# Two attention layers: new order of units and transfers, causal masks on VectorE, running mean on GpSimd

## The reference, cut to what matters

```python
# x: (16, 256, 128): 16 batches of 256 tokens of 128 channels; 16 heads of 8 channels
xn = layernorm(x)
q, k, v = heads(xn @ w_qkv + b_qkv)
attn = softmax(q @ k.T / sqrt(8) + rpe_bias)          # bias of (head, t - s), layer 0
s = (attn @ v) @ w_out + b_out
g = silu(mixture_of_experts(xn))                       # top 2 of 8 experts
x = x + s * g
xn = layernorm(x)
q, k = heads(xn @ qk_w + qk_b); v = heads(xn @ v_w)    # layer 1
attn = softmax(where(causal, q @ k.T / sqrt(8), -big))
new_attn = resid[h] * attn + skip[h] * eye - centre[h] * tril(1 / (t + 1))
s = (new_attn @ v) @ cproj_w
g = silu(xn @ W.T + b + (xn @ V_r) @ C.T)
x = x + s * g
```

## Time and profile before

| what | value |
|---|---|
| median of 3 runs | 1000.07 us (997.71 to 1005.07) |
| the profiled execution | 1001.72 us, span 999.9 us |
| TensorE (PE) busy | 786.2 us, 79% of the span |
| VectorE (DVE) busy | 645.5 us, 65% |
| ScalarE (ACT) busy | 509.3 us, 51% |
| GpSimd (POOL) busy | 411.4 us, 41% |
| DMA, mean | 106 GB/s, 106.13 MB |
| mean granted TensorE clock | 0.929 of full speed |

### The profile page before, as it was taken

How to read it: one execution, slowest core, us unless ns; L and a number is a source line. 1 busy time by engine, 2 the same in 40 slices (tenths; PEclk the granted TensorE clock), 3 DMA queues, 4 the chain that set the end, 5 groups by cost and what they waited for, 6 DMA issues and landing times.

```text
span 999.9 us, 19881 instructions
## 1 busy us (share of the span) xinstructions
PE 786.2 (79%) x6259; PEld 506.5 (51%) x6278; DVE 645.5 (65%) x1137; ACT 509.3 (51%) x883; POOL 411.4 (41%) x394
## 2 busy tenths in 40 slices
PE   0894787989988998854999999525598898989984
PEld 0652444555554554422555555314476666666663
DVE  6552786887788778832655655366356767676763
ACT  1243254676677766642433433258365555555542
POOL 7006776554555454421777777673210101010000
PEclk9996899999999999986999999856799999999997
DMA  5595745444544453142212222240665646464621
GB/s 141 194 192 138 174 121 123 97 94 102 123 115 92 100 122 88 31 136 59 58 53 53 58 55 54 78 122 16 142 135 124 148 117 159 115 157 117 136 58 51
DMA packets 132671, 106.13 MB, mean 106 GB/s; under 512 B 23317, under 2 KB 124633, under 8 KB 129545
## 3 DMA queue, kind: packets, MB, share of 16 engines
q1 hardware_dynamic: 122348, 91.23, 39.8%
q0 software_dynamic: 4352, 8.99, 2.9%
q10 hardware_dynamic: 5920, 5.24, 1.7%
HBM read 54.60 MB, written 50.03 MB: 105 GB/s over the span
## 4 chain that ended last, share of the span: by engine, by line
PE 27%; DMA 10%; DVE 7%; issue 4%; ACT 4%; SPq 2%; POOL 1%; DVEq 0%; ACTq 0%; POOLq 0%
PE ps L671 8%; DMA od_d<-ev 5%; PE ps L692 3%; PE ps L1567 3%; DVE mx L1272 3%; DMA rec<-od_d 2%; PE ps L683 2%; PE ps L665 2%; PE ps L1576 1%; ACT rows L893 1%; PE ps L673 1%; PE ps L1519 1%; SPq L1113 1%; PE ps L1517 1%; PE ps L1545 1%
## 5 line engine op out<-in xcount | busy, mean ns | idle before, releaser
L1272 DVE TENSOR_REDUCE mx<-ps 128x4 f32<-128x1024 f32 (+1 forms) x224 | 268.4, 1212 | 146.8 <-PE ps L1513 69.9
L1423 ACT ACTIVATE probs<-probs 128x1024 f32<-128x1024 f32 x128 | 131.8, 1051 | 64.9 <-DVE probs L1282 63.6
L1428 ACT ACTIVATE probs<-ps 128x1024 f32<-128x1024 f32 x96 | 96.8, 1024 | 82.9 <-PE ps L1545 55.8
L1202 POOL TENSOR_TENSOR qkr<-qkf,qk 128x512 f32<-128x512 f32 x27 | 31.3, 1160 | 244.0 <-ACT qk L1392 238.4
L1230 POOL TENSOR_TENSOR probs<-probs,tabB 128x1024 f32<-128x1024 f32 x42 | 99.5, 2369 | 74.6 <-ACT probs L1435 74.6
L1511 PE MATMUL ps<-tabA,eyeb 128*128 128x512 bf16 x256 | 102.3, 399 | 25.9 <-DMA ks<-parts_d 10.9
L1567 PE MATMUL ps<-probs,vpad 128*32 128x256 f32 (+1 forms) x2048 | 118.7, 362 | 4.2 <-ACT probs L1423 3.6
L1282 DVE TENSOR_TENSOR probs<-ps,tabB 128x1024 f32<-128x1024 f32 x86 | 101.5, 1210 | 4.3 <-PE ps L1539 4.3
L1513 PE MATMUL ps<-ks,qs 96*128 96x256 bf16 x512 | 102.3, 282 | 0.0
L1539 PE MATMUL ps<-qs,ks 99*128 99x256 bf16 x512 | 77.2, 280 | 6.8 <-DMA qs<-mT 2.6
L671 PE MATMUL ps<-qs,probs 128*128 x144 | 80.9, 644 | 1.4
(11 more groups left out here) (226 smaller groups left out, 1530.1 us busy)
## 6 DMA issues: line engine op xcount, KB each, us to landing
parts_d<-qk SPq DMA_DIRECT2D x64, 192.0 KB, 4.3
qs<-parts_d SPq DMA_DIRECT2D x32, 384.0 KB, 5.0
ks<-parts_d SPq DMA_DIRECT2D x32, 384.0 KB, 6.7
parts_d<-qk SPq DMA_DIRECT2D x64, 128.0 KB, 3.2
od_d<-ev SPq DMA_DIRECT2D x64, 128.0 KB
slots_in<-probs SPq DMA_DIRECT2D x1, 4680.0 KB
probs<-slots_in SPq DMA_DIRECT2D x72, 65.0 KB, 1.8
parts_d<-qk SPq DMA_DIRECT2D x64, 64.0 KB, 1.9
```

The lines of the kernel that those rows point to most:

```text
L1272: nc.vector.tensor_reduce(mx[:, s.buf(), t, heads[0]:heads[-1] + 1], ring[:, slot].rearrange("p (h n) -> p h n", n=w), AX.X, ALU.max).then ...
L1423: nc.scalar.activation(probs[:, j, :], probs[:, j, :], ACT.Exp).then_inc(exp_done, 1)
L1428: nc.scalar.activation(probs[:, j, :], ring[:, slot], ACT.Exp).then_inc(exp_done, 1)
```

## The change

Order of units: in layer 0 four A units now lead instead of three. The value products, the projections, V and the turned maxima stand at other places. The turn comes two units before the end of the period in layer 0 (`TURN` = 14). In layer 0 the units taken aside are 0, 2, 3 instead of 0, 2, 4, and unit 3's exponential comes after unit 6's. ScalarE copies the outputs later in layer 0 (place 7) and in layer 1 at place 4, behind the first B unit's exponential. SyncE's queue is reordered in both layers.

In layer 1 the mask of B units 0 to 3 is added by VectorE in PSUM (`causal`), and ScalarE waits for it. The resid gain is now in the weights of V, the skip gain is a factor in the addition, and the centre gain is multiplied once into `share`; so one product of the tokens serves both the skip term and the running mean, and it comes at place 7 of the order instead of 6, the additions on VectorE at 8. GpSimd makes the token copy, the scale, the multiplication and addition of the running mean, the parts of the maxima and the residual addition.

```diff
@@ Units
-        self.order = [("A", 0), ("A", 1), ("A", 2)]
-        for j in range(count - 3):
-            self.order += [("B", j), ("A", j + 3)]
+        self.order = [("A", j) for j in range(lead)]
+        for j in range(count - lead):
+            self.order += [("B", j), ("A", j + lead)]
@@ attention
-    U = Units(8 if layer == 0 else 6)
+    U = Units(8, 4) if layer == 0 else Units(6, 3)
...
-    LATE = 2 if layer else 4
-    SCALE = 2 if layer else 0
-    INVERT = 7 if layer else 10
-    VALUES = {9: (0, 1)} if layer else {13: (0, 1), 15: (2, 3)}
-    ASIDE = () if layer else (0, 2, 4)
-    ORDER = tuple(range(NU)) if layer else (1, 0, 3, 2, 5, 6, 4, 7)
-    PROJECT = 10 if layer else 8
+    LATE = {2: (2, 3), 4: (4, 5)} if layer else {3: (2, 3), 6: (4, 5), 8: (6, 7)}
+    VALUES = {8: (0, 1)} if layer else {12: (0, 1)}
+    SCALE, INVERT, PROJECT = (None, 11, 11) if layer else (9, 15, 11)
+    QK, V, TURN = (3, 5, NU * 2) if layer else (1, 5, 14)
+    ASIDE = () if layer else (0, 2, 3)
+    ORDER = tuple(range(NU)) if layer else (1, 0, 2, 4, 5, 6, 3, 7)
+    A_PART, A_OUT, A_TWO, A_VAL, A_MAX = (3, 4, 4, 4, 10) if layer else (4, 7, 5, 5, 12)
+    SEQ = ((("take", 0),), (("exp", 1),), (("take", 2), ("exp", 0)), (("take", 3), ("exp", 2)), (("exp", 4),),
+           (("exp", 5),), (("exp", 6), ("exp", 3)), (("exp", 7),))
@@ SyncE, body (conditions on the step left out)
-  stacks, parts 0, outputs_out, parts 1, sums_in, outputs_in, parts 2, inverses_out, inverses_in, maxima
+  layer 0: stacks, parts 0, 1, 2, outputs_out, sums_in, outputs_in, maxima, inverses_out, inverses_in
+  layer 1: stacks, parts 0, outputs_out, parts 1, 2, sums_in, outputs_in, maxima, inverses_out, inverses_in
@@ GpSimd
+            def second_body(s):
+                if s.has():
+                    tokens(s)
+                if s.has(2):
+                    rest_one(pool, nc.gpsimd, s)
+                if s.has(-3):
+                    scale(s)
+                if s.has(2):
+                    rest_two(pool, nc.gpsimd, s)
+                if s.has(-3):
+                    running_mean(s)
+                if s.has():
+                    parts_gpsimd(pool, s)
+                if s.has(-3):
+                    residual(s)
             def body(s):
+                if s.has() and s.k >= HELP:
+                    tokens(s)
...
+                    if n == 2 and s.has():
+                        parts_gpsimd(pool, s)
@@ VectorE
             def add_shape(s):
                 dve.wait_ge(e_full, s.n(-3) + 1)
+                nc.vector.tensor_tensor_scan(cum[:], v.onesT[:], misc[:, 0:T], 0.0, ALU.mult, ALU.add).then_inc(e_evac, 1)
                 dve.wait_ge(on_done, s.n(-3) + 1)
...
-                nc.vector.tensor_tensor(cum[:], cum[:], v.share, ALU.mult).then_inc(shaped, 1)
-                dve.wait_ge(shaped, n + 1)
-                nc.vector.tensor_tensor(on[:], on[:], cum[:], ALU.add).then_inc(shaped, 1)
+                nc.vector.scalar_tensor_tensor(on[:], misc[:, 0:T], cols[:, 5:6], on[:], ALU.mult, ALU.add
+                                               ).then_inc(e_evac, 1)
+            def causal(s, j, slot):
+                dve.wait_ge(full["B"], NU * s.n(-1) + j + 1)
+                diagonal = ring[:, slot].rearrange("p (h n) -> p h n", n=T)[:, :, 0:P]
+                nc.vector.tensor_tensor(diagonal, diagonal, maskB[:].unsqueeze(1).broadcast_to([P, 4, P]), ALU.add
+                                        ).then_inc(masked, 1)
@@ ScalarE, exponential of layer 1
-                    act.wait_ge(full["B"], NU * s.n(-1) + j + 1)
+                    if j < 4:
+                        act.wait_ge(masked, 4 * s.n(-1) + j + 1)
+                    else:
+                        act.wait_ge(full["B"], NU * s.n(-1) + j + 1)
@@ TensorE
-                elif w == T:
-                    if n % 2 == 0:
-                        diagonal = o[:, T * n:T * n + 2 * T].rearrange("p (h t) -> p h t", t=T)[:, :, 0:P]
-                        nc.tensor.matmul(diagonal, eyeb[:], maskB[:].unsqueeze(1).broadcast_to([P, 2, P]),
-                                         start=True, stop=False, skip_group_check=True)
...
-                        nc.tensor.matmul(misc[:, 0:T], v.wvs[:], batch_tokens(s, -3), start=True, stop=True)
-                        nc.tensor.matmul(misc[:, T:2 * T], v.wv1[:, 1, :], batch_tokens(s, -3), start=True, stop=True
-                                         ).then_inc(e_full, 1)
+                        nc.tensor.matmul(misc[:, 0:T], v.wv1[:], batch_tokens(s, -3), start=True, stop=True).then_inc(e_full, 1)
@@ middle, GpSimd
+        nc.gpsimd.tensor_scalar(v.share, v.share, v.cols[:, 6:7], None, ALU.mult).then_inc(cleared, 1)
```

More of the change, by code:

```diff
@@ L528, in _ @@
             pe.wait_ge(copied, 4 + 4 + 13)
-            for k in range(6):
+            for k in range(7):
                 nc.tensor.matmul(ps[:, 2, k:k + 1], rowsp[:, k, :], v.ones[0:1, 0:1], start=True, stop=True)
@@ L1257, in body @@
                     rest_two(pool, nc.gpsimd, s)
-                if layer == 0 and s.has() and s.k >= HELP:
-                    parts_gpsimd(pool, s)
             if layer:
                 ahead_of[1](pool)
-                pool.wait_ge(v.cleared, 4)
-                body(first)
-            emit(pool, body)
+                pool.wait_ge(v.cleared, 5)
+                second_body(first)
+            emit(pool, second_body if layer else body)
         @block.vector
@@ L1351, in body @@
                         scale(s)
+                    if layer and pos == 8 and s.has(-3):
+                        add_shape(s)
                     if U.exists(s.k, kind):
@@ L1356, in body @@
                             add_bias(s, j, U.slot(s.k, pos))
-                    if kind == "A" and j == NU - 1 and s.has() and (layer or s.k < HELP):
+                        elif layer and j < 4:
+                            causal(s, j, U.slot(s.k, pos))
+                    if kind == "A" and j == NU - 1 and s.has() and (layer == 0 and s.k < HELP):
                         maximum_parts(s)
-                    if layer and pos == 6 and s.has(-3):
-                        add_shape(s)
                     if pos == INVERT and s.has(-2):
@@ L1448, in body @@
             def body(s):
-                if s.has():
+                if layer == 0 and s.k < HELP and s.has():
                     if s.has(-1):
@@ L1453, in body @@
                 for pos, (kind, j) in enumerate(U.order):
-                    if pos == (0 if layer else 4) and s.has(-2):
+                    if pos == A_PART and s.has(2):
+                        parts_one(s)
+                    if pos == A_OUT and s.has(-2):
                         outputs(s)
                     if kind == "B" and U.exists(s.k, kind):
-                        if j in apart(s.k):
-                            take(s, j, U.slot(s.k, pos))
-                        else:
-                            exponential(s, j, U.slot(s.k, pos))
-                        if apart(s.k) and j in (2, 4, 6):
-                            exponential(s, j - 2, 0)
-                    if pos == 1 and s.has(2):
-                        parts_one(s)
-                    if pos == 4 and s.has(2):
+                        for what, i in (SEQ[j] if apart(s.k) else (("exp", j),)):
+                            if what == "take":
+                                take(s, i, U.slot(s.k, pos))
+                            else:
+                                exponential(s, i, U.slot(s.k, pos))
+                    if pos == A_TWO and s.has(2):
                         parts_two(s)
-                    if pos == 4 and s.has():
+                    if pos == A_VAL and s.has():
                         values(s)
+                    if pos == A_MAX and s.has():
+                        max_rows(s)
                 if layer and s.has(-3):
@@ L1474, in body @@
                     act.dma_start(v.wdn, v.down_w.rearrange("e (c i) h -> i e c h", c=2)).then_inc(v.w_load, 16)
-                if s.has():
+                if A_MAX >= len(U.order) and s.has():
                     max_rows(s)
@@ L1615, in body @@
                         mm.then_inc(y_full, 1)
+                    if pos == TURN and s.has():
+                        turn_maxima(s)
                     if U.exists(s.k, kind):
```

151 lines of the change are left out of this document (86 added, 65 removed).

## The result

| kernel | median, us | runs | ratio to before, 95% interval |
|---|---|---|---|
| before | 998.89 (995.75 to 1005.07) | 4 | |
| changed | 986.41 (984.3 to 987.07) | 4 | 0.9873, 0.9846 to 0.9900 |

The change makes the kernel 1.3% faster; 964 was forecast, with 944 to 984 as the range. The profiled execution took 984.3 us, its span was 982.5, so it is compared with 1001.7 and 999.9 of before.

What follows compares the result with a forecast made beforehand. Layer 0 was taken as bound by a ring of engine waits, changed layer 1 by its cycle of transfers; 1001.7 - 27 - 10 + 0.3 = 965 profiled, forecast as 964, range 944 to 984.

Steps and rivals of the forecast that it cites:

- Layer 0, -27: Layer 0: the new order shortens the period from 19.99 to 17.9 us; -27 us, between -10 and -38.
- Rival (3): Layer 0: VectorE's scale meets a GpSimd operation and waits, 1.5 us in 12 periods, so 982; chance 0.14.
- Layer 1, TensorE's work at 13.8: Layer 1, per period: fewer mask products and one token product less take TensorE from 15.1 to 13.8 us.
- Layer 1, the cycle of transfers at 15.95: Layer 1: transfers from maxima round to maxima bound the period, 15.95 us, taken as 16.0 against 16.78; layer -10.
- 1.43 for them to land: Layer 1's cycle: after their issue the inverses take 1.43 us to land and the broadcast back to go.
- The two small transfers ahead of the stacks have come in: Layer 1's cycle: inverses out and back now precede the stacks, which go out 3.2 us after the maxima.
- The end, +1.3: Layer 1's drain: scale, mean and residual on GpSimd are four operations at 0.74 instead of 0.41 us, +1.3.
- Rival (4): Layer 1 keeps its 16.8 us period, third parts and later stacks eating what left the cycle: 974; chance 0.12.
- Rival (5): SyncE's queue, both layers: outputs' issue to sums takes 8 us; layer 0 -5, layer 1 +24, 1020; chance 0.06.

Runs made afterwards that it cites:

- l0_new: Kernel before with the changed attention for layer 0 only, layer 1 and setup as before: 973.45 us, ratio 0.976.
- sp_old: Changed kernel with SyncE's order of before in layer 1 alone (third parts behind the outputs, inverses out and in ahead of the maxima): 967.69 us, ratio 0.971.
- before_pool: Kernel before with the last batch's residual addition on GpSimd and not on VectorE: 1004.1 us against 999.37, ratio 1.0044.
- mask_pe: Changed kernel with the masks of layer 1's units 0 to 3 made by TensorE again: 983.77 us, ratio 0.9844.
- gp_back: `sp_out_first` with layer 1's scale, running mean's two operations and residual back on VectorE from GpSimd: 963.77 us, ratio 0.9638.
- gp_back_pe: `gp_back` with the masks of layer 1's units 0 to 3 on TensorE again: 954.83 us, ratio 0.9545.
- mask_pe2: `sp_out_first` with the masks of layer 1's units 0 to 3 made by TensorE again: 959.47 us, ratio 0.9596.
- sp_out_first: Changed kernel with one line moved: layer 1's inverses are written out ahead of the maxima: 960.17 us, ratio 0.9628.
- gp_back_now: Changed kernel with layer 1's scale, running mean's two operations and residual back on VectorE from GpSimd: 989.55 us, ratio 0.9901.

## Why the prediction was wrong, step by step

- **Layer 0, -27.** Right in its mechanism, and a little lucky in its number: -27.6 in these two traces, but -24.1 between the medians of `l0_new`. From the first turn to the experts' first load the three traces with the old layer 0 take 350.6 to 352.1 and the fourteen with the new one 324.8 to 328.4, and the pair compared here is one end of each. The period is 17.87 for 17.9, the first periods held by GpSimd's gather and the token copy behind it, as said (V of the third period waited for it):

```profile
166.99 1.19 PE L1659 MATMUL ps<-wv,xb 128*128 128x128 f32 x4 [9.12 <-POOL xb L1270]
```

- **Rival (3), the scale against GpSimd.** Did not come: layer 0's scale takes 412/416/426 ns (least, median, most) over 16, against 1.29 in layer 1 of before. The rule of the Trainium skill (SBUF — State Buffer, section "SBUF: two separate sides"), that such a pair of operations exclude each other, is not contradicted by these durations: none of the sixteen ran beside an operation of GpSimd, the nearest of which ended 0.5 us before.
- **Layer 1, TensorE's work at 13.8.** Too low: it is busy 14.2 to 14.5 in periods at full clock, and no version has a period below 14.5 between turns 2 and 13. The forecast's own rows give 15.3 for the kernel before (16.78 less 1.23 and 0.23), not 15.1. It did not decide here.
- **Layer 1, the cycle of transfers at 15.95: the step that failed.** The mechanism was right, part by part: in the means of eleven periods stacks to sums takes 9.38 (9.34), sums to inverse 2.11 (2.0), inverse to maxima 1.58 (1.45). The mis-sized term is "1.43 for them to land", taken from a kernel where that write stood ahead of the maxima; behind them it took 2.21, and the hand-over to the stacks 0.91 for 0.65, so that the stacks went out at 4.12 for 3.2. These parts add up to 17.19 (measured 17.18), where the forecast's add up to 15.97 (it has 15.95) and it took 16.0. So eleven periods lost 13.0 against the forecast, 10.3 of it between the maxima and the stacks; the other 1.0 of the 14.0 that turns 0 to 13 lost lies in the first two periods, where no gain came. The lowered clock has a small part: in two of its four periods VectorE's inverse comes 1.1 and 1.2 ahead of the turn, and not 0.77. Undoing the order gave 15.38 (`sp_old`, which moves the third parts too), mending it by one line 15.04: the loss is the order's, shown.
- **"The two small transfers ahead of the stacks have come in", and were priced as a fixed 3.2.** The forecast did not ask whether the change's own order was a gain over the old one within the changed layer. It cost 16 to 19 us (0.9873 against 0.971, or 986.41 less 967.69): the old order in the new layer was the better kernel, and no rival said that.
- **The end, +1.3: measured +7.3.** Only GpSimd's slower operations were counted; GpSimd's `DRAIN` and the later value products stood at nothing. The traces give four parts: the end on GpSimd 3.9 (6.2 less 2.3; `before_pool` gave 4.4 by its ratio, with the slower addition in it), four operations and their hand-overs 0.7, 2.2 by which the last value products start later behind the last turn, 13.4 for 11.2, and 0.5 between ScalarE's copy and the outputs' issue, 1.9 for 1.3. The value products in the changed kernel (turn at 944.19), then in the kernel before (turn at 969.00):

```profile
957.56 1.95 PE L1628 MATMUL ps<-probs,vpad 128*32 128x256 f32 x48
```

```profile
980.17 1.95 PE L1567 MATMUL ps<-probs,vpad 128*32 128x256 f32 x48
```

  Ahead of each of their exponentials stands a mask's addition with nothing beside it: that this is the 2.2 fits `mask_pe`, where the masks leave VectorE and these products start at 11.2 again, and `gp_back` to `gp_back_pe`, where the end goes from 34.2 to 30.9, but not `mask_pe2`, whose end stayed at 37.6; it is the likely reason, not a shown one.
- **Rival (4), 974, was nearest** in its layer 1 period, but its reason (the third parts behind the outputs) was not the cause: with the same place of the parts, `sp_out_first` has 15.0.
- **Rival (5), the queue in both layers**, fell in layer 0 and came in a smaller form in layer 1: slower than before there, through the same queue.

## What to carry to other kernels

When a small write whose landing opens the next round is moved in a queue, price its landing by what now stands ahead of it, not by its own old row, and compare the new order with the old one inside the changed kernel. Where a cycle of transfers bounds the loop, one line of issue order was worth 24 to 26 us here, and moving arithmetic between engines that wait for that cycle was worth 3 us or less either way (`mask_pe`, `gp_back_now`). Once the order is mended, put the arithmetic where there is room: all three engines' loads, and the last batch's end, decide then. Before a transfer goes to a queue of its own, ask what its old place kept behind it.

## What the runs showed of the hardware beyond that

- An execution ended 6.2 us after GpSimd's last operation, whose `DRAIN` takes 5.97 of them (eleven traces), or 2.3 after VectorE's (six traces).
- An addition of 128x512 from PSUM and SBUF back into PSUM took 0.69 us on VectorE, a copy of 128x256 on GpSimd 0.40.
- In four periods of the changed kernel the granted clock fell to the lower level, 0.50, within 0.8 us of the end of a wait of TensorE of 2.54 to 2.94 us, and came back within the period.
- A 24 KB transfer on a second queue came 2.0 to 3.9 us too late when two of 384 KB were issued on the first ahead of it or at most 0.46 us behind it; 0.58 us or more behind it, only once in 28 periods, by 1.36.
